# Transposing x by DMA in place of TensorE and ScalarE in a recurrent block with an FP4 feed-forward part

## The chip, the core and the metric

The kernel runs on one core of a Trainium2 chip. The metric is the device time of one execution in microseconds (us). The engines are named as the profile names them: PE (TensorE; PEld is its weight load), DVE (VectorE), ACT (ScalarE), POOL (GpSimd) and SP (SyncE, which here only issues DMAs). They run their own instruction streams and meet at semaphores.

## The reference, cut to what matters

The input u has 8 sequences of 1024 rows of 256 features, so 8192 rows. Everything starts from the layer-normalised input xn.

```
x  = u
xn = layernorm(x)
s  = causal_conv(xn, k) + xn * D          # k: 128 taps for each of 256 features, from Lambda, dt, W
q(v) = blockwise FP4 round trip of v      # blocks of 16: scale = max|v| / 6, round to the FP4 grid
h  = silu(q(xn) @ q(w_gate).T) * (q(xn) @ q(w_up).T)      # 704 wide
g  = silu(q(h) @ q(w_down).T)
out = x + s * g
```

## The kernel before, in words

The 8192 rows are 64 tiles of 128 rows. A step of the main loop works on a pair of tiles, so there are 32 pairs, and one step more at the end to drain the pipeline (`NP = 32`; `it` is the step). Row tiles lie with rows on the partitions.

In step `it` the engines do the following.

- DVE quantises. It takes the block maxima (`largest`, L926) of 1920 columns at once: h of pair it-1 (two tiles of 704) and x of pair it+2 (two tiles of 256). Then come the scales (L933, L937), the reciprocals (L941), the division by the scale (`inverse`, L949), the two rounding passes (L963, L968), and the products with the scale in two f16 parts, high and low: `h_parts` (L1000) writes `hilo`, `x_parts` (L976) writes `xhl`. Between them it multiplies silu(gate) by up twice, `h_mult` (L992), for tiles 2it and 2it+1.
- PE takes the parts with rows on partitions and has to transpose them before they can be the weights of a product. `h_transpose` (L1365) does it for h, 11 blocks of 128x128 a tile. `x_transpose` (L1344) does it for x, 8 blocks a pair, from `xhl` into PSUM. `gate_up` (L1356) is 18 matmuls a tile, `down` (L1374, L1376) 17 a tile.
- ACT copies the transposed blocks from PSUM: `h_copy` (L688) and `x_copy` (L683, into `xT`). It also computes silu (L693, L697), squares for the rounding (L708), normalises x (`x_norm`, L676), and in the first quarter normalises and splits the convolution's copy of u (`a_scale` L659, `a_high` L670).
- POOL makes the scale tables that `h_parts` and `x_parts` read (`tables`, L516 to L534; semaphore `tb_p`), and in steps 0 to 7 the low parts of u (`a_low`, L539; it needs `a_high`'s result through `a_hi`).

The causal convolution is a Toeplitz product on PE, `conv` (L1389, L1393). A group is 8 features in two halves of 24 matmuls. It starts at step 8 (`S_CONV`), because it needs u's high and low parts of all 64 tiles. From step 8 to step 28 an even step has two groups and an odd step one. The Toeplitz blocks of a half are read from a padded copy of the filter in DRAM (`kpad`) by one DMA of 512 KB, `load_t` (L449), into one of two buffers `tpl`; the DMA of half n waits until half n-2 is done (`cv_h`). The filter itself gets into `kpad` by 16 small DMAs, `store_filter` (L442).

The order of the work is written out by hand in each engine's stream; there is no scheduler. SP's stream is in order too, so a DMA that waits holds up those behind it. SP issues, per step, the load of a pair of x (`load_x`, L405), in steps 0 to 6 a copy of one sequence from u to the output in DRAM (`copy_input`, L455), and from step 8 on the `load_t`s.

Before step 1 there is a set-up: the filter and the quantised, transposed weights are made, and pairs 0 and 1 go through by hand (`gate_up(0, ...)` and `gate_up(1, ...)`, L1433 and L1444; `weights_out`, L817, copies the transposed weights from PSUM).

In the lines below, `x_hl` counts finished products of `x_parts`, `x_tp` PE's transposes of x, `x_tc` ACT's copies of them, `gu_p` finished `gate_up`s, `h_v` finished `h_mult`s.

```
def x_copy(p, par):                         # ACT
    act.wait_ge(x_tp, p + 1)
    after(act, gu_p, p * 2 - 2)
    nc.scalar.copy(xT[par], p_xT).then_inc(x_tc, 1)
```

Of the kernel before, what the change touches and what calls it, by code (L numbers as in the profile page):

```python
# [17 lines left out]
P = 128  # L18
# [51 lines left out]
def build(nc, u, u_rev, D, Lre, Lim, logdt, Wre, Wim, wg, wu, wd, out):  # L70
# [5 lines left out]
    with ExitStack() as ctx:  # L76
# [149 lines left out]
        x_tc = sem("x_tc")  # L226
        t_in = [sem(f"t_in{i}") for i in range(2)]
# [173 lines left out]
        def _(sp):  # L401
# [36 lines left out]
            def store_filter():  # L438
                sp.wait_ge(k_split, 3)
                for part, src in enumerate((kh, kl)):  # L440
                    for a in range(8):
                        sp.dma_start(  # L442
                            bass.AP(kpad, part * 3 * P + P - 1 + 16 * a, [[16 * 6 * P, 16], [6 * P, 16], [1, 16]]),
                            src[a:P:FA, :].rearrange("p (g b) -> p g b", b=16)).then_inc(k_dram, 16)
# [21 lines left out]
            sp.wait_ge(k_dram, 16 * 16)  # L466
            sp.wait_ge(w_ca, 13)
            load_t(0, 0)
            sp.wait_ge(x_hl, 2 * S_CONV + 4)
            load_t(1, 1)  # L470
            with sp.Fori(0, PAIRS - 1) as q:
                for par in range(2):
                    load_x(q * 2 + (S_CONV + par + 3), 1 - par)
                    for k in range(4 - 2 * par):
                        load_t(q * 6 + (4 * par + k + 2), k % 2)
            for it in range(S_TAIL - 2, NP - 3):
                load_x(it + 3, (it + 1) % 2)
                for n in range(2 * groups_before(it) + 2, min(2 * groups_before(it + 1) + 2, H // 4)):
                    load_t(n, n % 2)
            for n in range(2 * groups_before(NP - 3) + 2, H // 4):  # L480
                load_t(n, n % 2)
# [8 lines left out]
        def _(pool):  # L490
# [140 lines left out]
            for it in range(NP + 1):  # L631
                tables(it, it < NP - 2, it >= 1)
                if it == 1:
                    pool.wait_ge(k_split, 2)
                    nc.gpsimd.tensor_tensor(kl, kt, kh, ALU.subtract).then_inc(k_split, 1)
                some_stores()
                if it < NP - 2:
                    pool.wait_ge(x_hl, 2 * (it + 3))
                elif it < NP:
                    pool.wait_ge(hl_v, it)  # L640
                if it < S_CONV:
                    a_low(it * 2)
                    a_low(it * 2 + 1)
# [10 lines left out]
        def _(act):  # L654
# [68 lines left out]
            def step(it, par, x, xt, xn, gu, ch, td, a2=False, cv=0, c0=None, td1=True, late=False, more=None):  # L723
# [14 lines left out]
                if xt:  # L738
                    x_copy(it + 1, 1 - par)
# [8 lines left out]
                if more is not None:  # L748
                    a_scale(more, 2)
# [113 lines left out]
            weights_out(range(8, 11))  # L863
            a_scale(15, 0, 2)
# [3 lines left out]
            x_copy(1, 1)  # L868
            weights_out(range(11, 13))
# [7 lines left out]
            for it in range(1, PEEL):  # L877
                step(it, it % 2, True, True, True, True, True, it >= 2, a2=True, td1=it >= 3, late=it == 1,
                     more=15 if it == 3 else None)
            with act.Fori(0, (S_CONV - PEEL) // 2) as q:  # L880
                for par in range(2):
                    step(q * 2 + (PEEL + par), par, True, True, True, True, True, True, a2=True)
# [605 lines left out]
```

## Time and profile before

| | us |
|---|---|
| time, median of 3 runs | 563.04 (562.21 to 564.03) |
| the profiled execution's own time | 563.28 |
| its span, first to last instruction | 561.5 |
| busy: PE, DVE, ACT, POOL | 478.2, 531.4, 404.7, 220.2 |

The profile is of one execution. The granted clock of PE was 0.977 of full speed in the mean over the span. Busy times of PE are modelled at their ends, so a busy PE is not one at its peak. Steps are read off DVE's stream: each begins with one L926.

### The profile page before, as it was taken

The numbers are of one execution on the slowest core, as the hardware profiler recorded it, in microseconds if no ns is written. First come the engines' busy times: TensorE is split into PE (matmuls) and PEld (weight loads), VectorE is DVE, ScalarE is ACT, GpSimd is POOL, SyncE is SP. The second block draws the span as 40 slices with busy tenths as digits, with TensorE's granted clock in tenths as the row PEclk, the third lists the DMA queues.
The fourth block names the chain that finished last, engine by engine and source line by source line (L and its number), as shares of the span: only waits on it lengthen the run. The fifth ranks groups of instructions, "written<-read, shape, count | busy, mean of one in ns | idle before, by whom it ended". The sixth has DMA issues, their size and how long they took to land.

```text
span 561.5 us, 13319 instructions
## 1 busy us (share of the span) xinstructions
PE 478.2 (85%) x4981; PEld 332.7 (59%) x4981; DVE 531.4 (95%) x685; ACT 404.7 (72%) x571; POOL 220.2 (39%) x328
## 2 busy tenths in 40 slices
PE   0003487689989999999999999999999999999996
PEld 0000444255555567777777777777777777776675
DVE  6999999899999999999999999999999999999987
ACT  6959789879888876666766666666666767666554
POOL 1399832845544541111111111133332333337770
PEclk9999859799999999999999999999999999999999
DMA  5990005152221046253535353435353544426998
GB/s 164 351 321 1 1 20 187 23 175 95 95 94 54 5 134 187 77 171 94 152 99 147 96 160 97 140 95 168 95 169 95 144 122 126 139 76 134 191 175 178
DMA packets 101956, 70.82 MB, mean 126 GB/s; under 512 B 8864, under 2 KB 101536, under 8 KB 101792
## 3 DMA queue, kind: packets, MB, share of 16 engines
q1 hardware_dynamic: 94624, 62.73, 38.0%
q0 software_dynamic: 7280, 7.34, 8.6%
q8 instruction: 40, 0.66, 0.5%
q14 instruction: 12, 0.10, 0.1%
HBM read 61.28 MB, written 16.12 MB: 138 GB/s over the span
## 4 chain that ended last, share of the span: by engine, by line
PE 62%; DVE 26%; issue 6%; ACT 3%; POOL 2%; DMA 0%; SPq 0%; DVEq 0%; ACTq 0%; POOLq 0%
PE ps L1356 32%; PE ps L1374 10%; PE ps L1376 5%; PE ps L1365 5%; PE ps L1389 4%; PE ps L1393 4%; DVE work L968 3%; DVE work L1052 3%; DVE work L963 2%; DVE sm L926 2%; DVE work L992 2%; PE ps L1344 2%; DVE xh L1030 2%; DVE work L1000 1%; DVE work L976 1%
## 5 line engine op out<-in xcount | busy, mean ns | idle before, releaser
L1356 PE MATMUL ps<-wgu,work 128*128 128x512 f16 (+1 forms) x1152 | 243.9, 367 | 15.2 <-DVE work L992 15.0
L1356 PEld LDWEIGHTS ps<-wgu,work 128*128 128x128 f16 x1152 | 110.2, 99 | 126.6 <-issue 14.0
L693 ACT ACTIVATE work<-ps,con 128x704 f32<-128x704 f32 x64 | 54.3, 848 | 96.4 <-PE ps L1356 96.3
L1374 PE MATMUL ps<-wdh,work 128*128 128x256 f16 x704 | 87.2, 272 | 0.3 <-ACT work L688 0.2
L688 ACT COPY work<-ps 128x1408 f16<-128x1408 f16 x64 | 84.9, 1327 | 2.8 <-PE ps L1365 2.7
L549 POOL TENSOR_TENSOR gbuf<-gbuf,xh 128x256 f32<-128x256 f32 (+1 forms) x42 | 37.8, 930 | 94.0 <-DVE work L976 86.8
L963 DVE SCALAR_TENSOR_TENSOR work<-work 128x960 f32<-128x960 bf16 (+2 forms) x67 | 72.5, 1119 | 0.3 <-ACT work L708 0.2
L949 DVE TENSOR_TENSOR work<-work,ps 128x960 f32<-128x960 f32 (+2 forms) x67 | 71.4, 1105 | 1.2
L968 DVE SCALAR_TENSOR_TENSOR work<-work 128x1920 f16<-128x1920 bf16 (+3 forms) x36 | 69.7, 1936 | 1.2
L1374 PEld LDWEIGHTS ps<-wdh,work 128*128 128x128 f16 x704 | 65.3, 98 | 7.6 <-ACT work L688 0.4
L926 DVE TENSOR_REDUCE sm<-work 128x120 f32<-128x1920 f32 (+2 forms) x33 | 68.0, 2059 | 1.3
L708 ACT ACTIVATE work<-work 128x960 bf16<-128x960 f32 (+2 forms) x67 | 61.9, 960 | 3.4 <-DVE work L949 2.8
L1000 DVE TENSOR_TENSOR work<-work,sm 128x1408 f16<-128x1408 f16 (+1 forms) x66 | 54.9, 873 | 8.6 <-DVE work L968 5.0
L516 POOL TENSOR_SCALAR sm<-sm 128x2 int32<-128x2 int32 x32 | 8.5, 265 | 138.6 <-DVE sm L937 138.6
L992 DVE TENSOR_TENSOR work<-work,ps 128x704 f32<-128x704 f32 x64 | 56.4, 881 | 5.6 <-ACT work L693 5.5
L539 POOL TENSOR_TENSOR xh<-gbuf,xh 128x1024 f16<-128x1024 f32 x16 | 38.8, 2445 | 47.1 <-ACT xh L670 26.6
L697 ACT ACTIVATE gbuf<-ps,sm 128x256 f32 (+1 forms) x64 | 30.3, 474 | 32.9 <-PE ps L1376 32.8
L1365 PE MATMUL ps<-id,work 128*128 128x128 f16 x704 | 49.8, 219 | 4.5 <-DVE work L1000 4.3
L1376 PE MATMUL ps<-wdl,work 128*128 128x256 f16 x384 | 52.4, 273 | 0.0
L1365 PEld LDWEIGHTS ps<-id,work 128*128 128x128 f16 x704 | 43.2, 98 | 12.8 <-DVE work L1000 7.0
L1389 PE MATMUL ps<-xh,work 128*128 128x64 f16 x768 | 50.3, 192 | 0.0
L1393 PE MATMUL ps<-xh,work 128*128 128x56 f16 x768 | 50.1, 191 | 0.0
(156 smaller groups left out, 685.7 us busy)
## 6 DMA issues: line engine op xcount, KB each, us to landing
work<-kpad SPq DMA_DIRECT2D x64, 512.0 KB, 3.8
gbuf<-u_rev SPq DMA_DIRECT2D x4, 2048.0 KB, 18.7
work<-L_attn_u SPq DMA_DIRECT2D x32, 256.0 KB, 3.4
out<-gbuf POOLq DMA_DIRECT2D x7, 1024.0 KB, 11.5
work<-L_attn_u SPq DMA_DIRECT2D x1, 1024.0 KB, 5.5
out<-gbuf SPq DMA_DIRECT2D x3, 256.0 KB, 3.0
work<-L_ffn_w_down SPq DMA_DIRECT2D x1, 704.0 KB, 6.6
work<-L_ffn_w_gate SPq DMA_DIRECT2D x1, 640.0 KB, 4.6
```

Of the source, the lines that this page charges most:

```text
L688: nc.scalar.copy(hT[par], src).then_inc(hT_a, 1)
L926: own.mark(V.tensor_reduce(bm[:, cols], by_blk[pp][:, cols], AX_X, ALU.max, apply_absolute_value=True))
L949: V.tensor_tensor(v, v, sc, ALU.mult).then_inc(v_v, 1)
L963: own.mark(V.scalar_tensor_tensor(v, d_bf[:, c], C0, v, ALU.add, ALU.subtract))
L968: return V.scalar_tensor_tensor(r_f16[:, c], d_bf[:, c], C0, by_blk[pp][:, c], ALU.add, ALU.subtract)
L992: V.tensor_tensor(vb[par][:, I * t:I * t + I], sg, p_gu[:, I:2 * I], ALU.mult).then_inc(h_v, 1)
L1356: last = T.matmul(p_gu[:, a:b], xT[par][:, t, c, :], wgu[:, part, c % 2, a:b], start=(n == 0), stop=(n == len(todo) - 1))
L1365: last = T.transpose(dst[:, c, :], hilo[par][:, t, c * P:c * P + P], id16[:])
L1374: T.matmul(dst, hT[t][:, c, :], wdh[:, c, :], start=(c == 0), stop=False)
L1376: last = T.matmul(dst, hT[t][:, c, :], wdl[:, c, :], start=False, stop=(c == RT - 1))
L1389: T.matmul(dst, tpl[half][:, 2 * c + tp, 0:P], col[:, xp, :], start=(n == 0), stop=False)
L1393: last = T.matmul(dst1, tpl[half][:, 2 * c + tp, P:2 * P], before, start=False, stop=(n == 2))
```

## The change

x is no longer transposed by PE and copied by ACT, except for pair 0. SP issues a transposing DMA from `xhl` to `xT` for pair it+1 in its part of step it (`x_transpose` on SP, for pairs 1 to 31). It waits for the products of x (`x_hl`) and for the `gate_up`s that still read that `xT` buffer (`gu_p`). `gate_up` waits for the DMA (`x_td`, one semaphore for each of the two buffers) in place of `x_tc`, and so does `x_parts` before it overwrites `xhl`, in place of `x_tp`. SP's loop over steps is written out. The 16 stores of the filter go out four each in SP's steps 2 to 5, each four behind the transposing DMA of their step.

In the set-up ACT copies the last two blocks of transposed weights before `silu_gate(1)`; the two halves of `a_scale(15)` become one in step 2, so `a_high(0)` and `a_high(1)` stand right behind `silu_gate(1)`. PE transposes these two blocks before `gate_up(1)`. POOL's subtraction for the filter's low part stands behind its wait for x of step 1.

```
@@ sync
+            def x_transpose(p):
+                sp.wait_ge(x_hl, p * 2 + 2)
+                after(sp, gu_p, p * 2 - 2)
+                sp.dma_start_transpose(xT[p % 2].rearrange("p t c k -> p (t c) k"),
+                                       xhl[p % 2].rearrange("p t c -> p (t c)")).then_inc(x_td[p % 2], 16)
...
-            for it in range(PEEL):
-                load_x(it + 3, (it + 1) % 2)
-                if it == 2:
-                    store_filter()
-                copy_input(it)
-            for it in range(PEEL, S_CONV):
-                load_x(it + 3, (it + 1) % 2)
-                copy_input(it)
             sp.wait_ge(k_pad, 32)
...
+            for it in range(NP - 1):
+                if it < NP - 3:
+                    load_x(it + 3, (it + 1) % 2)
+                if it == 0:
+                    sp.wait_ge(k_all, 1)
+                if it == S_CONV - 1:
+                    sp.wait_ge(k_dram, 16 * 16)
+                    sp.wait_ge(w_ca, 13)
+                    load_t(0, 0)
+                x_transpose(it + 1)
+                if 2 <= it < 6:
+                    store_filter(it // 2 - 1, it % 2 * 4)
+                if it < S_CONV:
+                    copy_input(it)
+                if it == S_CONV:
+                    load_t(1, 1)
+                if it >= S_CONV:
+                    for n in range(2 * groups_before(it) + 2, min(2 * groups_before(it + 1) + 2, H // 4)):
+                        load_t(n, n % 2)
@@ gpsimd
                 tables(it, it < NP - 2, it >= 1)
-                if it == 1:
-                    pool.wait_ge(k_split, 2)
-                    nc.gpsimd.tensor_tensor(kl, kt, kh, ALU.subtract).then_inc(k_split, 1)
                 some_stores()
                 if it < NP - 2:
                     pool.wait_ge(x_hl, 2 * (it + 3))
                 elif it < NP:
                     pool.wait_ge(hl_v, it)
+                if it == 1:
+                    pool.wait_ge(k_split, 2)
+                    nc.gpsimd.tensor_tensor(kl, kt, kh, ALU.subtract).then_inc(k_split, 1)
@@ scalar, step
+                if more is not None:
+                    a_scale(more)
...
-                if xt:
-                    x_copy(it + 1, 1 - par)
...
-                if more is not None:
-                    a_scale(more, 2)
@@ scalar, set-up
-            weights_out(range(8, 11))
-            a_scale(15, 0, 2)
+            weights_out(range(8, 13))
             square(0, 1, True, False, 0)
             x_norm(3, 1)
             silu_gate(1)
-            x_copy(1, 1)
-            weights_out(range(11, 13))
             a_high(0, 2)
@@ vector, x_parts
-                after(dve, x_tp, p - 1)
+                if isinstance(p, int) and p < 3:
+                    after(dve, x_tp, p - 1)
+                else:
+                    dve.wait_ge(x_td[par], (p - 2 + par) * 8)
@@ tensor, gate_up
-                    pe.wait_ge(x_tc, first)
+                    if first == 1:
+                        pe.wait_ge(x_tc, 1)
+                    else:
+                        pe.wait_ge(x_td[par], (first - 1 + par) * 8)
@@ tensor, step
-                if x:
-                    x_transpose(it + 1, 1 - par)
@@ tensor, set-up
-            gate_up(1, 1, 0, None)
-            pe.wait_ge(con_ok, 1)
-            x_transpose(1, 1)
             pe.wait_ge(w_ca, 9)
             transposed_down(3)
             pe.wait_ge(w_ca, 10)
             transposed_down(4)
+            gate_up(1, 1, 0, None)
```

How the streams move, at the places that matter. Rows name the line, the operation, output and inputs, and in brackets the semaphores that it waits for; `ps` is PSUM, `work` the scratch area that holds `xhl`, `xT`, `hilo` and `tpl`.

PE, a step with convolution, from the last matmuls of its first `gate_up` to the first half of a group, before:

```order
L1356 MATMUL ps<-wgu,work 128x512 x2
L1356 MATMUL ps<-wgu,work 128x384
L1344 MATMUL ps<-id,work 128x128 [waits hT_a,x_tc,x_hl]
L1344 MATMUL ps<-id,work 128x128 x7
L1389 MATMUL ps<-xh,work 128x64 [waits cv_e,t_in0,a_lp]
L1389 MATMUL ps<-xh,work 128x64 x2
L1393 MATMUL ps<-xh,work 128x8x7 x3
```

The same place now:

```order
L1360 MATMUL ps<-wgu,work 128x512 x2
L1360 MATMUL ps<-wgu,work 128x384
L1391 MATMUL ps<-xh,work 128x64 [waits cv_e,t_in0,a_lp]
L1391 MATMUL ps<-xh,work 128x64 x2
L1395 MATMUL ps<-xh,work 128x8x7 x3
```

The eight transposes and their three waits are gone, and the convolution follows the `gate_up` directly.

SP, from the last `copy_input` to the second step with convolution, before (the stream is then a loop, so registers stand between):

```order
L455 DMA out<-L_attn_u 16x16384
L405 DMA work<-L_attn_u 128x2x256 [waits x_r]
L449 DMA work<-kpad 128x8x256 [waits w_ca,k_dram,k_pad]
L449 DMA work<-kpad 128x8x256 [waits x_hl]
L471 UNCONDITIONAL_BRANCH
L471 ISA
L405 ISA [waits x_r]
L405 DMA work<-L_attn_u 128x2x256
```

The same place now:

```order
L456 DMA out<-L_attn_u 16x16384
L406 DMA work<-L_attn_u 128x2x256 [waits x_r]
L450 DMA work<-kpad 128x8x256 [waits w_ca,k_dram]
L462 DMA_TRANSPOSE work<-work 128x8x128 [waits gu_p,x_hl]
L406 DMA work<-L_attn_u 128x2x256 [waits x_r]
L462 DMA_TRANSPOSE work<-work 128x8x128 [waits gu_p,x_hl]
L450 DMA work<-kpad 128x8x256
L450 DMA work<-kpad 128x8x256 [waits cv_h] x4
```

In each step one transposing DMA stands behind the step's `load_x` and ahead of its `load_t`s.

ACT, the end of the set-up, from the first `silu_gate` to the splitting of the filter, before:

```order
L693 ACTIVATE work<-ps,con 128x704 [waits gu_p,w_h,w_lo]
L822 COPY wdh<-ps 128x1024 [waits w_tr] x2
L822 COPY wdh<-ps 128x768 [waits w_tr]
L659 ACTIVATE gbuf<-gbuf,sm 128x256 x2
L708 ACTIVATE work<-work 128x512 [waits v_v,x_hl]
L676 ACTIVATE work<-work,nmr,rstd 128x256 [waits x_in1]
L676 ACTIVATE work<-work,nmr,rstd 128x256
L693 ACTIVATE work<-ps,con 128x704 [waits h_v,gu_p]
L683 COPY work<-ps 128x1024 [waits x_tp]
L822 COPY wdl<-ps 128x1024 [waits w_tr]
L822 COPY wdl<-ps 128x512 [waits w_tr]
L670 ACTIVATE xh<-gbuf 128x4x128x2 [waits w_ca,k_max,a_xs]
```

The same place now:

```order
L696 ACTIVATE work<-ps,con 128x704 [waits gu_p,w_h,w_lo]
L823 COPY wdh<-ps 128x1024 [waits w_tr] x2
L823 COPY wdh<-ps 128x768 [waits w_tr]
L823 COPY wdl<-ps 128x1024 [waits w_tr]
L823 COPY wdl<-ps 128x512 [waits w_tr]
L711 ACTIVATE work<-work 128x512 [waits v_v,x_hl]
L679 ACTIVATE work<-work,nmr,rstd 128x256 [waits x_in1]
L679 ACTIVATE work<-work,nmr,rstd 128x256
L696 ACTIVATE work<-ps,con 128x704 [waits h_v,gu_p]
L673 ACTIVATE xh<-gbuf 128x4x128x2 [waits w_ca,k_max,a_xs]
```

`a_high(0)` (the last row of each) now follows the second `silu_gate` with nothing between.

## Rows read from the trace of the kernel before

**Rows 1.** Page, part 1: busy time and share of each engine.

```profile
PE 478.2 (85%) x4981; PEld 332.7 (59%) x4981; DVE 531.4 (95%) x685; ACT 404.7 (72%) x571; POOL 220.2 (39%) x328
```

**Rows 2.** Windows: stretch, length; busy PE, PEld, DVE, ACT, POOL; PE's clock, DMA share.

```profile
124.57:196.67 72.10, 65.03 (x500) 41.86 (x500) 69.91 (x76) 65.28 (x94) 38.24 (x46) 1.00 0.22 73
225.62:518.58 292.96, 292.30 (x3404) 212.04 (x3401) 281.09 (x301) 198.28 (x270) 78.74 (x174) 1.00 0.45 124
```

**Rows 3.** Timeline of DVE, steps 10 to 30: start, length, line [idle before it].

```profile
225.62 2.15 DVE L926 TENSOR_REDUCE sm<-work 128x120 f32<-128x1920 f32 x1
...
298.54 2.15 DVE L926 TENSOR_REDUCE sm<-work 128x120 f32<-128x1920 f32 x1
304.72 0.89 DVE L992 TENSOR_TENSOR work<-work,ps 128x704 f32<-128x704 f32 x1 [0.36 <-ACT work L693]
313.50 2.15 DVE L926 TENSOR_REDUCE sm<-work 128x120 f32<-128x1920 f32 x1
319.23 0.88 DVE L992 TENSOR_TENSOR work<-work,ps 128x704 f32<-128x704 f32 x1
324.64 1.69 DVE L1000 TENSOR_TENSOR work<-work,sm 128x1408 f16<-128x1408 f16 x2 [0.20 <-DVE work L968]
327.84 2.15 DVE L926 TENSOR_REDUCE sm<-work 128x120 f32<-128x1920 f32 x1
...
518.58 1.62 DVE L926 TENSOR_REDUCE sm<-work 128x88 f32<-128x1408 f32 x1
```

**Rows 4.** Chain of waits, from step 16: start, length, line and instructions.

```profile
313.56 0.61 PE ps L1365 x11
314.17 3.56 PE ps L1356 x18
317.74 0.45 PE ps L1344 x8
318.18 0.09 PE ps L1389 x3
...
318.89 1.20 PE ps L1374 x11
320.10 0.66 PE ps L1376 x6
...
342.86 0.61 PE ps L1365 x11
```

**Rows 5.** Timeline of DVE, steps 1 and 2.

```profile
92.93 2.15 DVE L926 TENSOR_REDUCE sm<-work 128x120 f32<-128x1920 f32 x1
...
105.90 2.17 DVE L1000 TENSOR_TENSOR work<-work,sm 128x1408 f16<-128x1408 f16 x2 [1.68 <-POOL sm L531]
...
109.65 2.15 DVE L926 TENSOR_REDUCE sm<-work 128x120 f32<-128x1920 f32 x1
```

**Rows 6.** Timeline of POOL, step 1.

```profile
95.10 4.85 POOL L539 TENSOR_TENSOR xh<-gbuf,xh 128x1024 f16<-128x1024 f32 x2 [6.12 <-ACT xh L670]
99.91 1.14 POOL L516 TENSOR_SCALAR sm<-sm 128x2 int32<-128x2 int32 x1
...
105.23 0.64 POOL L531 TENSOR_TENSOR sm<-sm 128x240 f16<-128x240 f32 x1
```

**Rows 7.** Timeline of ACT, end of the set-up.

```profile
91.35 0.99 ACT L683 COPY work<-ps 128x1024 f16<-128x1024 f16 x1
...
93.86 2.08 ACT L670 ACTIVATE xh<-gbuf 128x1024 f16<-128x1024 f32 x2
```

**Rows 8.** Timeline of PE: `gate_up(2)` and `gate_up(3)`.

```profile
92.97 3.73 PE L1356 MATMUL ps<-wgu,work 128*128 128x512 f16 x18 [1.94 <-DVE work L992]
...
99.60 5.24 PE L1356 MATMUL ps<-wgu,work 128*128 128x512 f16 x18 [2.46 <-DVE work L992]
```

**Rows 9.** Page, part 6: DMA issues, KB each, us from issue to landing.

```profile
work<-kpad SPq DMA_DIRECT2D x64, 512.0 KB, 3.8
```

**Rows 10.** DMA issues by line: the padding's zeros, 512 rows of 254 bytes.

```profile
kpad<-work SPq DMA_DIRECT2D x1, 127.0 KB, 6.8
```

More of the change, by code:

```diff
@@ L226, in build @@
         x_tc = sem("x_tc")
+        x_td = [sem(f"x_td{i}") for i in range(2)]
         t_in = [sem(f"t_in{i}") for i in range(2)]
@@ L436, in _, with store_filter @@
             load_x(2, 0)
-            def store_filter():
+            def store_filter(part, a0):
                 sp.wait_ge(k_split, 3)
[L440 to L444, printed above, removed]
+                src = (kh, kl)[part]
+                for a in range(a0, a0 + 4):
+                    sp.dma_start(
+                        bass.AP(kpad, part * 3 * P + P - 1 + 16 * a, [[16 * 6 * P, 16], [6 * P, 16], [1, 16]]),
+                        src[a:P:FA, :].rearrange("p (g b) -> p g b", b=16)).then_inc(k_dram, 16)
             def load_t(n, par):
@@ L721, in y_copy, with step @@
                                      scale=con[:, C_CONV:C_CONV + 1]).then_inc(cv_e, 1)
-            def step(it, par, x, xt, xn, gu, ch, td, a2=False, cv=0, c0=None, td1=True, late=False, more=None):
+            def step(it, par, x, xn, gu, ch, td, a2=False, cv=0, c0=None, td1=True, late=False, more=None):
                 if td:
@@ L877, in _ @@
             for it in range(1, PEEL):
-                step(it, it % 2, True, True, True, True, True, it >= 2, a2=True, td1=it >= 3, late=it == 1,
-                     more=15 if it == 3 else None)
+                step(it, it % 2, True, True, True, True, it >= 2, a2=True, td1=it >= 3, late=it == 1,
+                     more=15 if it == 2 else None)
             with act.Fori(0, (S_CONV - PEEL) // 2) as q:
                 for par in range(2):
-                    step(q * 2 + (PEEL + par), par, True, True, True, True, True, True, a2=True)
+                    step(q * 2 + (PEEL + par), par, True, True, True, True, True, a2=True)
             act.wait_ge(con_ok, 1)
@@ L885, in _ @@
                 for par in range(2):
[L886 removed]
+                    step(q * 2 + (S_CONV + par), par, True, True, True, True, True, cv=2 - par, c0=q * 3 + 2 * par)
             for it in range(S_TAIL, NP - 2):
[L888 to L890 removed]
+                step(it, it % 2, True, it < NP - 3, True, True, True, cv=groups_of(it), c0=groups_before(it))
+            step(NP - 2, 0, False, False, True, True, True)
+            step(NP - 1, 1, False, False, True, True, True)
             h_copy(NT - 4, 0)
@@ L1358, in gate_up, with h_transpose @@
                 last.then_inc(gu_p, 1)
-            def h_transpose(n, t, par, dst=p_hT, copied=None):
+            def h_transpose(n, t, par, dst=p_hT):
                 after(pe, hT_a, n if dst is p_hT else n - 1)
-                if copied is not None:
-                    pe.wait_ge(x_tc, copied)
                 for c in range(NC11):
@@ L1399, in keep_running, with step @@
                     T.matmul(ps[:, 1024:1024 + H], id16[:], wdh[:, n % NC11, :], start=True, stop=True)
-            def step(it, par, x, gu, td, cv=0):
+            def step(it, par, gu, td, cv=0):
                 if td:
                     pe.wait_ge(hl_v, it - 1)
-                    h_transpose(it * 2 - 4, 0, par, copied=min(it + 1, NP))
+                    h_transpose(it * 2 - 4, 0, par)
                 if gu:
                     gate_up(it * 2, 0, par, it + 1)
-                if x:
-                    x_transpose(it + 1, 1 - par)
                 if cv:
@@ L1418, in step @@
                 if td:
-                    h_transpose(it * 2 - 3, 1, par, copied=it + 2 if x else None)
+                    h_transpose(it * 2 - 3, 1, par)
                 if cv == 2:
@@ L1450, in _ @@
             transposed_down(4)
+            gate_up(1, 1, 0, None)
             for it in range(1, NP - 1):
-                step(it, it % 2, True, True, it >= 2, groups_of(it) if it >= S_CONV else 0)
-            step(NP - 1, 1, False, True, True)
-            step(NP, 0, False, False, True)
+                step(it, it % 2, True, it >= 2, groups_of(it) if it >= S_CONV else 0)
+            step(NP - 1, 1, True, True)
+            step(NP, 0, False, True)
             down(NT - 3, 1, p_dn2)
```

20 lines of the change are left out of this document (removed).

## The prediction, made before the changed kernel ran

> **What bounds the kernel now.** I read the page's busy shares first, then windows over the stages, then DVE's timeline (how long is a step?) and the chain of waits (who sets it?), and last POOL, ACT and PE in the set-up. The page alone points at DVE: 95% busy against PE's 85% [rows 1]. The windows split that. In steps 3 to 7 (124.57 to 196.67) the five steps take 72.10 us, 14.42 each, with DVE busy 97% and PE 90% [rows 2]: DVE is the bound there, and PE work taken away saves nothing. From 225.62 to 518.58, steps 10 to 29, PE is busy 292.30 of 292.96 us and DVE 96% [rows 2]: PE is the bound, but DVE is close behind.
>
> How close is what the estimate hangs on. DVE's timeline shows steps in turns of two lengths: step 16 from 313.50 to 327.84 is 14.34 us, step 15 from 298.54 to 313.50 is 14.96. In the long one `h_mult` waits 0.36 us for silu, and so for a late `gate_up`; in the short one there is no wait before it [rows 3]. So 14.34 us is DVE's own length. A pair of steps takes 292.96 / 10 = 29.30 us now, and 28.68 would be DVE's floor. The chain of waits says the same from the other side: it runs on PE alone from 313.56 to 342.86, 29.30 us with no gap [rows 4].
>
> **The convolution steps.** PE loses the eight transposes, 0.45 us a step [rows 4], so its pair falls from 29.30 to 28.40 us. That is under DVE's 28.68, so DVE becomes the bound and the gain is 29.30 - 28.68 = 0.62 a pair, not 0.90: over ten pairs 292.96 - 20 x 14.34 = 6.2 us.
>
> Does DVE really run free, when PE has only 0.28 us a pair to spare and its two steps are unequal? An even step has two groups. A half of a group is eight rows of 0.09, so 0.71 us; `h_transpose` is 0.61, `gate_up` 3.56, `down` 1.86 [rows 4]. The even step is then 2 x 0.61 + 2 x 3.56 + 2 x 1.86 + 4 x 0.71 = 14.9 us on PE, the odd one two halves less, 13.5. If DVE's even step begins at S, `gate_up` may start at S + 0.1 (the last `h_mult` frees the PSUM bank), its `h_transpose` being done before, and PE ends the step at S + 14.4. DVE's odd step begins at S + 14.34; PE transposes h for 0.61, runs `gate_up` for 3.56, silu takes 0.85, so DVE can multiply 5.2 us after its step began. It wants to at 319.23 - 313.50 = 5.73 [rows 3]. There is 0.5 us to spare, so the 0.36 us waits go. The second `gate_up` of a step has more room.
>
> **ACT and DVE.** ACT loses a copy of 1.0 us a step [rows 7]. It is busy 68% in these steps [rows 2] and is not what anyone waits for, so I count nothing. In its loop DVE's wait before `x_parts` is now for a number worked out in a register of its own. The nearest row for what that can cost is the 0.20 us of idle before `h_parts`, which also waits for a computed number behind its own last result [rows 3]. Lower bound 0, upper bound 0.20 a step over 26 looped steps, 5.2 us. I take 0: the number can be worked out while the second product of `h_parts` runs, and that takes 0.85 of the 1.69 us [rows 3].
>
> **The transposing DMA.** No DMA of this kind is in the trace. It moves 256 KB in 1024 rows of 256 bytes. The nearest rows are `load_t`, 512 KB in 1024 rows of 512 bytes, 3.8 us to landing [rows 9], and the padding's zeros, 512 rows of 254 bytes, 6.8 us for half the bytes [rows 10], which would give 13.6. Lower end 1.9 (half of `load_t`), upper end 13.6; I take 4, because `load_t` has the same number of rows and runs in the same steps on the same queue, while the zeros went out beside 8 MB of u. It is issued when `x_parts` is done, one `h_mult` (0.9) before DVE's next step, or when the last `load_t` of the step is off SP, which is PE's end of the step. Its reader, `gate_up` of the next step but one, comes a whole step (14.3 us) later. At 4 us nobody waits, and even 13.6 would just do.
>
> The tighter customer is the next `load_t`, which lies behind it in the queue. In an even step the first `load_t` can go when the first half is done, S + 0.1 + 3.56 + 0.71 = S + 4.4, which is 5.3 us after the DMA was issued at S - 0.9. Its Toeplitz blocks are wanted by the second group, S + 11.1, so it has 6.7 us for its 3.8, 2.9 to spare. The transposing DMA may therefore hold the queue for 8.2 us before PE waits.
>
> Two pages of the Trainium skill bear on this and disagree. "VectorE: DVE Perf Modes", section "The three transpose paths", gives 1309 ns for one 128x128 block by DMA and 390 ns on TensorE, and its rules prefer TensorE where PSUM will do; if the eight blocks went one after the other, that would be an estimated 10.5 us, 2.3 past the point, and would speak against the change. In this trace a block costs PE 0.45 / 8 = 0.056 us in a stream [rows 4], far less than the page's figure, so its figures are not those of a stream. "Advanced Engine Details and Errata", section "X-Bar Transpose (TRN2)", says that such DMAs are as fast as regular ones, which would put it at or below the 4 us taken. No run here yet shows which holds.
>
> **The filter's stores and POOL.** The 16 stores move from one block to four steps, behind transposing DMAs; `kpad` is first read in step 7's part of SP, more than a step after the last of them. Nothing.
>
> **The set-up.** Step 1 takes 16.72 us and step 2 follows at 109.65 [rows 5]; steps 3 to 7 average 14.42 [rows 2], so step 1 has 2.3 us too much. 1.68 of them are DVE waiting for POOL's tables before `h_parts` [rows 5]. POOL is late because `a_low`, 4.85 us, starts only at 95.10, when `a_high(0)` is through ACT, and the tables come behind it from 99.91 to 105.87 [rows 6]. ACT begins `a_high` at 93.86, after `x_copy` at 91.35 and the two weight copies [rows 7]. Now it begins at about 91.4, 2.4 us earlier. POOL then starts its tables at 97.5 and, at the 5.96 us that they take now, ends by 103.5, before DVE asks at 105.90 - 1.68 = 104.2. So the 1.68 us go. The weight copies land in ACT's idle time and before `silu_gate(1)`; PE's `gate_up(1)` begins some 1.2 us later behind the two weight blocks and its silu is then just in time. What replaces the stall: `gate_up(2)` now waits for the first transposing DMA, issued at about 87.8; at 4 us it lands before the 92.97 at which `gate_up(2)` starts now [rows 8], and DVE needs its result only 1 us after it is there. The rest of the 2.3 us is DVE work slowed beside POOL's, which partly goes. I take 2.0; ends 0 and 2.8.
>
> **Sum.** 6.2 + 2.0 = 8.2 us off the profiled execution's 563.28 (the closing steps, with DVE waiting once for silu, I leave at nothing): 555.1. The median of the runs is 0.24 lower, so 554.9 us.
>
> **Rivals.** (a) *The DMA holds the queue* (slower). By the zeros' row it would take 13.6 us, 5.4 past the 8.2 at which it decides. PE would wait that once a pair: 28.40 + 5.4 = 33.8 against 29.30, ten times, 45 us more, less 2: about 606 us. Just past the point, at 9.2 us, PE's pair is 29.4 and nothing is gained but the set-up. For it: rows of 256 bytes, a kind of DMA that no row shows. Against: `load_t` with as many rows in 3.8. At the page's estimated 10.5 us it would be 2.3 late, a pair of 30.7, and some 575 us.
> (b) *DVE pays for the computed wait*, 0.1 us in each of 26 steps: 2.6 less, 557.5; at 0.20, 560.1. For it: DVE is the bound everywhere afterwards, so nothing hides it.
> (c) *The set-up gives nothing back.* PE's clock: `gate_up(3)` took 5.24 us after 2.46 us of idle, `gate_up(2)` 3.73 after 1.94 [rows 8]; the same instructions at 1.2 and 2.4 GHz in part. PE now has less work before `gate_up(2)` and a longer gap; if that one is slow too, DVE waits about 0.6, and the same in step 2: gain 6.2 or less, 556.9.
> (d) *PE stays the bound* because the slack of 0.28 us a pair isn't usable, and pairs stay at 29.0 or above: 3 + 2 off, 558; with the set-up lost too, no change.
>
> **How the numbers follow.** Forecast 0.62, (a) 0.10, (b) 0.12, (c) 0.10, (d) 0.06. The forecast's own range is 552.5 to 557: the set-up's 0 to 2.8 and half a microsecond of spread. To leave out no more than 2 in 10 I go up to 560.0, which takes in (b), (c) and most of (d), and down to 552.0; (a) is left out. A run of this kernel tells a difference from none at about 0.3%, 1.7 us. Slower by more than that is (a), 0.10 less the part of it that ends near today's time, plus a little for what I didn't see: 0.09. Within it: 0.05. Faster: 0.86.
>
> **What would show it.** Right: DVE's steps 10 to 29 all at 14.34 us, no `h_mult` waiting for silu, PE busy about 97% there with its gaps before `gate_up`; L1000 in step 1 without the wait for POOL; the transposing DMA at 3 to 5 us, `load_t` still near 4. Wrong: convolution matmuls waiting for `work<-kpad` or `gate_up` for the transposing DMA (a), even and odd steps both a little over 14.34 with an idle before `x_parts` (b), `gate_up(2)` over 5 us (c), pairs still uneven (d).

## The result, and the profile after

The changed kernel takes 554.79 us in the median of four runs (554.51 to 555.17), where the kernel before takes 563.5 in the four runs made beside them (562.21 to 564.03). The ratio is 0.9853, with a 95% interval of 0.9838 to 0.9867, so the change is worth 1.5%. The forecast was 554.9. The profiled execution's own time is 554.96 us, and its span is 553.2. Of the experiments' executions below, one of e1's twelve took 1768 us and is in no ratio, and two of e11's seven took 558.2 and 559.5 where its other five lie within 0.5 us.

The page's first part, to be read beside [rows 1]. DVE keeps its 685 instructions and about its busy time, while PE, ACT and POOL lose some:

```profile
PE 466.3 (84%) x4733; PEld 318.7 (58%) x4733; DVE 529.0 (96%) x685; ACT 379.6 (69%) x540; POOL 218.1 (39%) x328
```

Windows over step 1 and over steps 10 to 29, with the columns of [rows 2]:

```profile
93.11:107.94 14.83, 10.29 (x47) 4.81 (x47) 14.15 (x16) 10.14 (x17) 8.72 (x11) 0.85 0.41 124
223.22:509.77 286.55, 284.67 (x3238) 202.64 (x3235) 279.27 (x301) 183.12 (x250) 77.77 (x174) 1.00 0.57 142
```

The last window took 292.96 us before and takes 286.55 now. DVE's busy time in it has fallen by only 1.8 us, from 281.09 to 279.27, while its share rose from 96% to 97.5%. PE still shows 99%, with 166 recorded matmuls fewer. Its idle time in the window rose only from 0.66 to 1.88 us, which is 0.19 a pair, and as the ends of matmuls are modelled this is a rough figure. The share says little on which engine sets the step. The stretches between starts on DVE say it.

DVE's timeline, steps 16 and 17, to be read against [rows 3]:

```profile
309.18 2.15 DVE L924 TENSOR_REDUCE sm<-work 128x120 f32<-128x1920 f32 x1
...
314.92 0.88 DVE L993 TENSOR_TENSOR work<-work,ps 128x704 f32<-128x704 f32 x1
...
320.33 1.69 DVE L1001 TENSOR_TENSOR work<-work,sm 128x1408 f16<-128x1408 f16 x2 [0.20 <-DVE work L966]
...
323.53 2.15 DVE L924 TENSOR_REDUCE sm<-work 128x120 f32<-128x1920 f32 x1
...
337.84 2.15 DVE L924 TENSOR_REDUCE sm<-work 128x120 f32<-128x1920 f32 x1
```

The step's first instruction, `largest`, stands 14.35 and 14.31 us from the next one. `h_mult` (L993) begins 5.74 us after it, with no wait in brackets, and 5.73 us after it in the next step. The long step of [rows 3], in which it stood 0.36 us for silu, is gone. The short one has stayed as it was.

The chain of waits, with its shares by engine from the page's fourth part:

```profile
DVE 61%; issue 22%; PE 11%; ACT 3%; DVEq 1%; POOL 1%; DMA 0%; SPq 0%; ACTq 0%; POOLq 0%
```

Its pieces over one step, first and last, in the place of [rows 4]:

```profile
309.18 2.16 DVE sm L924
...
323.53 2.17 DVE sm L924
```

Where [rows 4] run on PE from `h_transpose` to `h_transpose`, these run on DVE from `largest` to `largest`. The bound has moved from PE to DVE.

The span is 8.3 us shorter. Cut at DVE's step starts, the difference is made up like this:

| Stretch | Before | After | Difference | Forecast |
|---|---|---|---|---|
| start to step 3 | 124.57 | 122.65 | -1.9 | -2.0 |
| steps 3 to 9 | 101.05 | 100.57 | -0.5 | 0 |
| steps 10 to 29 | 292.96 | 286.55 | -6.4 | -6.2 |
| steps 30 and 31 up to the last `largest` | 24.03 | 23.77 | -0.3 | 0 |
| from there to the end (the span is given to 0.1) | 18.9 | 19.7 | +0.8 | 0 |

In the last of these stretches DVE does its work in the same time. Its last instruction starts 16.2 us after that `largest` in both traces (542.61 before, 533.54 after):

```profile
558.85 0.42 DVE L1249 TENSOR_TENSOR gbuf<-gbuf,work 128x256 f32<-128x256 f32 x1
...
549.77 0.42 DVE L1250 TENSOR_TENSOR gbuf<-gbuf,work 128x256 f32<-128x256 f32 x1
```

Behind it stand only the last stores. The span ends 2.2 us after DVE's last instruction before (561.5 - 559.3) and 3.0 us after it now (553.2 - 550.2). That is the 0.8.

The first row of the table, the set-up, sets one execution against one. In e7, e8, e9 and e10, whose programs are the same up to here, step 3 begins at 123.02, 123.29, 123.31 and 122.80 us, where it begins at 122.65 in this trace. So by traces the gain is 1.3 to 1.9 us, and this trace is the best of five.

The set-up, on the three engines of the forecast. First DVE, against [rows 5], with the window of step 1 before:

```profile
92.93:109.65 16.72, 10.20 (x55) 4.90 (x55) 14.80 (x16) 14.03 (x21) 12.66 (x11) 0.89 0.28 92
...
99.28 0.89 DVE L993 TENSOR_TENSOR work<-work,ps 128x704 f32<-128x704 f32 x1 [0.34 <-ACT work L696]
...
104.68 1.69 DVE L1001 TENSOR_TENSOR work<-work,sm 128x1408 f16<-128x1408 f16 x2
```

The 1.68 us that `h_parts` waited for POOL are gone, and a new wait of 0.34 for silu has come. Of the 1.89 us by which step 1 is shorter, 1.24 are idle time of DVE and 0.65 its busy time, which fell from 14.80 to 14.15: `h_parts`, for one, takes 1.69 us and no longer the 2.17 of [rows 5]. POOL, against [rows 6]:

```profile
92.94 4.83 POOL L542 TENSOR_TENSOR xh<-gbuf,xh 128x1024 f16<-128x1024 f32 x2 [3.78 <-ACT xh L673]
97.74 0.22 POOL L519 TENSOR_SCALAR sm<-sm 128x2 int32<-128x2 int32 x1
...
99.57 0.64 POOL L534 TENSOR_TENSOR sm<-sm 128x240 f16<-128x240 f32 x1
```

`a_low` starts 2.16 us earlier, because `a_high(0)` does on ACT, at 91.71 where [rows 7] have 93.86:

```profile
91.71 2.05 ACT L673 ACTIVATE xh<-gbuf 128x1024 f16<-128x1024 f32 x2
```

PE's `gate_up(2)` and `gate_up(3)`, against [rows 8]:

```profile
93.16 5.20 PE L1360 MATMUL ps<-wgu,work 128*128 128x512 f16 x18 [2.47 <-DVE work L993]
...
100.22 3.74 PE L1360 MATMUL ps<-wgu,work 128*128 128x512 f16 x18 [1.87 <-DVE work L993]
```

The slow one is now `gate_up(2)`, with 5.20 us for the 18 matmuls that took 3.73 before, and DVE's 0.34 us are the wait for its silu. The window over it has the clock in the third column from the end, 0.71 of full speed:

```profile
93.11:98.40 5.29, 5.20 (x18) 2.04 (x18) 5.18 (x6) 1.46 (x4) 5.15 (x4) 0.71 0.98 297
```

The transposing DMAs and, for e9 below, the closing transfers, from the DMA issues (KB each, where given, and median us to landing), beside [rows 9]:

```profile
work<-kpad SPq DMA_DIRECT2D x64, 512.0 KB, 4.1
...
work<-L_attn_u SPq DMA_DIRECT2D x1, 1024.0 KB, 12.7
out<-gbuf SPq DMA_DIRECT2D x3, 256.0 KB, 4.0
...
work<-work SPq DMA_TRANSPOSE x31, 3.2
```

They land after 3.2 us in the median: 18 of the 31 after 3.0 to 3.7, 12 after 4.7 to 6.6 and the last one, in step 30, after 10.7. The mean is 4.2. Even the last is in time, landing at 519.6 for a step that starts at 521.3. The `load_t` behind them rose only from 3.8 to 4.1.

### The profile page after: what moved, and what is told of

Its sections match the earlier page's. It is cut to its first block, busy times and chain, and to the rows that moved or that the text cites. A ratio compares the mean times of both kernels' runs of the same rounds, so it can differ in the third digit from the quotient of the medians.

```text
span 553.2 us, 12607 instructions
## 1 busy us (share of the span) xinstructions
PE 466.3 (84%) x4733; PEld 318.7 (58%) x4733; DVE 529.0 (96%) x685; ACT 379.6 (69%) x540; POOL 218.1 (39%) x328
## 4 chain that ended last, share of the span: by engine, by line
DVE 61%; issue 22%; PE 11%; ACT 3%; DVEq 1%; POOL 1%; DMA 0%; SPq 0%; ACTq 0%; POOLq 0%
DVE work L966 11%; DVE sm L924 10%; DVE work L961 9%; PE ps L1360 7%; DVE work L993 6%; DVE ps L939 4%; DVE work L977 3%; DVE work L1053 3%; DVE work L947 3%; DVE work L1001 2%; DVE xh L1031 2%; DVE sm L931 1%; PE ps L1376 1%; DVE xh L1021 1%; PE ps L1367 1%
## 5 line engine op out<-in xcount | busy, mean ns | idle before, releaser
L993 DVE TENSOR_TENSOR work<-work,ps 128x704 f32<-128x704 f32 x64 | 56.3, 880 | 2.0 <-ACT work L696 1.8
L1391 PEld LDWEIGHTS ps<-xh,work 128*128 128x128 f16 x768 | 43.8, 96 | 5.2 <-POOL xh L542 0.9
## 6 DMA issues: line engine op xcount, KB each, us to landing
work<-L_attn_u SPq DMA_DIRECT2D x1, 1024.0 KB, 12.7
```

The source lines that it names most:

```text
L993: V.tensor_tensor(vb[par][:, I * t:I * t + I], sg, p_gu[:, I:2 * I], ALU.mult).then_inc(h_v, 1)
L1391: T.matmul(dst, tpl[half][:, 2 * c + tp, 0:P], col[:, xp, :], start=(n == 0), stop=False)
```

## The experiments

Twelve kernels ran. Eleven are edits of the changed kernel, and `setup_only` (e4) is an edit of the kernel before. A ratio is always to the kernel before.

**e1 and e5, TensorE's work alone.** This asks whether the gain in the steps is PE's relief and nothing else. Eight constant transposes of the identity go back on PE in e1, two in e5. x still comes by DMA.

```diff
+                if 1 <= it < NP - 1:
+                    after(pe, hT_a, it * 2 - 3)
+                    for n in range(8):       # 2 in e5, 16 in e6
+                        T.transpose(p_xT[:, n // 4 % 2, n % 4, :], id16[:], id16[:])
```

> The changed kernel, with eight transposes of a constant block put back on TensorE in steps 1 to 30, where x's stood; ScalarE's copy stays out and x still comes by DMA. Theory (TensorE was the bound in the convolution steps, and its 0.45 us a step is what was gained): pairs of steps back from 28.65 to 29.30 us, 561.2 us (560.5 to 561.8). Rival (the gain came from ScalarE's missing copy, or from x being there a step early): 554.8.

Measured: 561.87 us, ratio 0.9971 (0.996 to 0.9983). DVE's timeline in e1:

```profile
295.86 2.15 DVE L924 TENSOR_REDUCE sm<-work 128x120 f32<-128x1920 f32 x1
302.11 0.89 DVE L993 TENSOR_TENSOR work<-work,ps 128x704 f32<-128x704 f32 x1 [0.44 <-ACT work L696]
...
310.80 2.15 DVE L924 TENSOR_REDUCE sm<-work 128x120 f32<-128x1920 f32 x1
```

The long step of 14.94 is back with its wait for silu, and steps 10 to 29 take 292.96 us, exactly as before. Nothing of ACT's part, of the DMAs or of the set-up was undone. So the 6.4 us of the steps are PE's eight transposes. What e1 still has over the kernel before, 1.6 us, is about the set-up's gain.

> The changed kernel with two constant transposes a step on TensorE where x's stood. Theory (TensorE now has 28.65 - 28.40 = 0.25 us to spare in a pair, and two times 0.11 us fit in): no change, 554.8 us (554.3 to 555.5). Rival (every TensorE instruction still costs its own time): 20 x 0.11 = 2.2 more, 557.0.

Measured: 555.16 us, 0.9843 (0.9826 to 0.9859), with steps of 14.34 and 14.32. Two blocks on PE in each step, 0.11 us, cost nothing. So PE's time to spare can be used.

**e6, sixteen transposes.** If DVE's 28.65 us a pair is a floor and PE's length a straight line that crosses it, sixteen must cost what eight cost and 0.45 a step more.

> The changed kernel with sixteen constant transposes a step on TensorE. Theory (over the spare 0.25 us every us on TensorE costs a us): a pair is 28.40 + 1.80 = 30.20 us, ten pairs 15.5 more, 570.3 us (569 to 572). Rival (latencies between the engines add to it): 575 or more.

Measured: 571.26 us, 1.0133 (1.0116 to 1.015), with steps of 14.41 and 15.78, 30.19 a pair. DVE's wait in the long step has grown to 1.27 us:

```profile
305.97 0.89 DVE L993 TENSOR_TENSOR work<-work,ps 128x704 f32<-128x704 f32 x1 [1.27 <-ACT work L696]
```

The pair goes 28.65 (none), 28.66 (two), 29.30 (eight), 30.19 (sixteen): flat at first, and 0.89 between eight and sixteen, which is the 16 x 0.056 of the added blocks. Taken back from 29.30 at that slope, PE's own pair without transposes is 28.4, as forecast, and DVE's floor is met at about two blocks a step.

**e2, ScalarE's copy put back.** A copy of the same size, of constant data, at the same place on ACT, and `silu_gate` behind it.

```diff
+                if gu and xn:
+                    act.wait_ge(h_v, it * 2 + 1)
+                    nc.scalar.copy(sg.bitcast(F16)[:, 0:1024].rearrange("p (c k) -> p c k", c=8),
+                                   id16[:].rearrange("p (o k) -> p o k", o=1).to_broadcast([P, 8, P])).then_inc(x_dm, 1)
```

> The changed kernel, with a copy of 128x1024 f16 (about 1 us) put back on ScalarE in steps 1 to 28, at the old place of x's copy; its result is not used. Theory: ScalarE is busy two thirds and nobody waits for it, so 554.8 us (554.3 to 555.6). Rival (its copy was in the way of silu or of the convolution's copies): 557 or more.

Measured: 554.89 us, 0.9847 (0.9827 to 0.9866). The window of steps 10 to 29:

```profile
223.57:510.24 286.67, 284.72 (x3238) 202.22 (x3235) 279.38 (x301) 198.76 (x269) 77.54 (x174) 1.00 0.57 142
```

ACT is busy 198.76 us in it, as much as before the change (198.28 in [rows 2]), and the window is 0.12 us longer. ACT's copy was worth nothing, as counted.

**e3 and e4, the set-up.** e3 is the changed kernel with the orders of u's high parts, of the weight copies, of `gate_up(1)` and of the filter's subtraction as before. e4 is the kernel before with these orders alone changed.

```diff
 # e3, core of the edit
-            weights_out(range(8, 13))
+            weights_out(range(8, 11))
+            a_scale(15, 0, 2)
...
+            weights_out(range(11, 13))
...
-                     more=15 if it == 2 else None)
+                     more=15 if it == 3 else None)
```

> The changed kernel with the set-up's order of before (weight copies and half a_scale ahead of a_high, transposed_down behind gate_up(1), GpSimd's subtraction first); x comes by DMA. Theory (the first step's gain is GpSimd's tables coming in time, because a_high starts earlier): a_high starts 1.5 us later than now, 0.7 earlier than before, so the tables are late by 0.5 to 1 us: 555.7 us (555.0 to 556.8). Rival (the first step gained because TensorE's and ScalarE's work on x is gone there): 554.8.

Measured: 556.56 us, 0.9875 (0.9854 to 0.9896), 1.8 us over the changed kernel. POOL and DVE are as in [rows 5, 6] again, in small. POOL:

```profile
94.23 4.84 POOL L542 TENSOR_TENSOR xh<-gbuf,xh 128x1024 f16<-128x1024 f32 x2 [5.31 <-ACT xh L673]
```

and DVE's `h_parts` behind it:

```profile
104.94 2.17 DVE L1003 TENSOR_TENSOR work<-work,sm 128x1408 f16<-128x1408 f16 x2 [0.53 <-POOL sm L534]
```

The wait is 0.53 and not 1.68 us, since `a_low` begins at 94.23 and not at 95.10: the x copy of [rows 7] is gone from ahead of `a_high` on ACT. So a part of the gain here, some 0.9 us of POOL's start, comes with the transposing DMA. The 1.8 us aren't all the tables' either. Against the changed kernel, step 1 of e3 is 0.98 us longer (15.81), with the wait and the slower `h_parts`, and step 2 is 0.60 longer (15.31), with a wait of 0.82 for silu behind a slow `gate_up(4)`. Such a wait stands in e2 too (1.19 in step 2), which has the new orders, so it isn't shown to come from the old ones.

> The kernel before with only the set-up's new order; x is still transposed by TensorE and copied by ScalarE. Theory: a_high starts 1.5 us earlier than before, the 1.7 us wait for GpSimd's tables goes, 1.8 us less: 561.7 us (561.0 to 562.5), and steps 10 to 29 stay at 29.30 us a pair. Rival: the set-up's order alone does nothing, 563.5.

Measured: 561.48 us, 0.997 (0.9958 to 0.9982). Steps 1 and 3 begin here:

```profile
92.41 2.15 DVE L924 TENSOR_REDUCE sm<-work 128x120 f32<-128x1920 f32 x1
...
103.95 1.70 DVE L998 TENSOR_TENSOR work<-work,sm 128x1408 f16<-128x1408 f16 x2
...
121.93 2.15 DVE L924 TENSOR_REDUCE sm<-work 128x120 f32<-128x1920 f32 x1
```

The orders alone take the wait away. Step 3 begins 2.6 us before the 124.57 of the kernel before, but takes 15.20 us itself where it took 14.23, so that 1.75 us are left at step 10. Steps 10 to 29 keep their 14.35 and 14.94. The two halves add up: e4 is 2.0 us under the kernel before, the changed kernel 7.1 under e1, and together that is 9.1 where 8.7 was measured for both.

**e7 and e8, how long SP's queue may be held.** Rival (a) was a condition, a queue held for more than 8.2 us. In even steps one (e7) or two (e8) stores of 1.41 MB follow the transposing DMA, from a buffer that nobody writes to one that nobody reads.

```diff
+                if 10 <= it <= 28 and it % 2 == 0:
+                    for n in range(1):       # 2 in e8
+                        sp.dma_start(spill[it * 1 + n], wgu[:, :, :, :].rearrange("p a k c -> p (a k c)")).then_inc(x_sp, 16)
```

> The changed kernel with one store of 1.41 MB from SBUF to an unused DRAM buffer behind the transposing DMA in the ten even steps 10 to 28; it holds the queue. Theory (the next load of filter blocks has 8.2 us from the issue of the transposing DMA before TensorE waits; the two DMAs together hold it for about 8): 0 to 3 us more, 554.8 to 558. Rival (what lies ahead in the queue does not delay a load): 554.8 here and in the run with two stores.

Measured: 553.93 us, 0.9828 (0.9812 to 0.9845). SP's timeline:

```profile
308.76 1.23 SPq L464 DMA_TRANSPOSE work<-work  x1
310.03 0.58 SPq L480 DMA_DIRECT2D spill<-wgu  x1
314.14 2.92 SPq L452 DMA_DIRECT2D work<-kpad  x2
```

This store lands 5.2 us after its issue, 310.03 + 5.2 - 308.76 = 6.5 us after the transposing DMA went out. In the ten pairs it is 6.5 to 8.4 us, and the first `load_t` lands 9.0 to 10.3 us after the transposing DMA. That costs nothing. The first `load_t` goes out 5.4 us after the transposing DMA, where 5.3 was forecast.

> As the run before with two stores, 2.8 MB. Theory: the queue is held for about 14.5 us, 6 past the point, once a pair in ten pairs: 60 us more, 615 us (590 to 640). Rival: 554.8.

Measured: 572.88 us, 1.0169 (1.0152 to 1.0186): slower, but far less than expected. SP's timeline:

```profile
315.11 1.23 SPq L464 DMA_TRANSPOSE work<-work  x1
316.38 1.06 SPq L480 DMA_DIRECT2D spill<-wgu  x2
320.54 9.74 SPq L452 DMA_DIRECT2D work<-kpad  x3
```

The landing of the 20 stores:

```profile
DMA to landing us min/median/max: 5.2/7.9/10.5
```

And what PE's weight loads waited for in the steps (us in all, times, longest), with the wait of this pair:

```profile
PEld ps L1397 <- DMA work<-kpad: 17.8, 12, 2.4
...
329.01 0.14 PEld L1397 LDWEIGHTS ps<-xh,work 128*128 128x128 f16 x3 [1.93 <-DMA work<-kpad]
```

The median of the landings is no store's own: the first of a pair lands after 5.2 to 6.7 us, the second after 9.0 to 10.5. Counted from the transposing DMA the second is there after 10.9 to 12.4 us. I had assumed 14.5, and that is one part of the miss. The other is that `load_t` doesn't take its 3.8 us behind the last store: it lands only 1.5 to 3.4 us after it, 12.7 to 14.3 after the transposing DMA. In this pair that is 13.9 us (329.01 - 315.11).

PE asks for it at 329.01 - 1.93 = 327.08, which is 12.0 us after the transposing DMA. The forecast had 8.2 + 3.8 = 12.0. The price follows from there: the stretch from step 10 to step 29 is 303.3 us, 16.7 over the changed kernel's, so 1.7 a pair, between 0.9 and 3.5. So the mechanism and its point are right when the landing of `load_t` is the measure: 10.3 us cost nothing and 12.7 cost a wait. As a time for which the queue is held, the 8.2 us are only bounded, between 8.4 us that cost nothing in e7 and 10.9. That a transposing DMA which lands as late would have cost the same is argued; no run has one in these pairs.

**e9, the closing stretch.** It lost 0.8 us. In the changed kernel the load of u's last rows (1 MB) waits behind the last transposing DMA. e9 puts it ahead.

```diff
+                if it == NP - 2:
+                    sp.wait_ge(cv_h, H // 4)
+                    sp.dma_start(u_last, u_t[:, NT - 8:NT, :]).then_inc(u_in, 16)
...
-            sp.wait_ge(cv_h, H // 4)
-            sp.dma_start(u_last, u_t[:, NT - 8:NT, :]).then_inc(u_in, 16)
```

> The changed kernel with the last load of u (1 MB, for the closing sums) ahead of the last transposing DMA in SP's stream and no longer behind it. Theory (the tail lost 0.8 us because this load slid from 57 to 41 us before the end, into the time of GpSimd's accumulating stores, and the last stores land in 3.0 and no longer 2.2 us): 0.8 us less, 554.0 us. Rival (the landing varies by itself, or by the stores alone): 554.8.

Measured: 554.53 us, 0.9844 (0.9826 to 0.9862). The DMA issues:

```profile
work<-L_attn_u SPq DMA_DIRECT2D x1, 1024.0 KB, 5.5
out<-gbuf SPq DMA_DIRECT2D x3, 256.0 KB, 2.2
```

The load lands in 5.5 us instead of 12.7, the closing stores in 2.2 instead of 4.0, and the stretch takes 18.9 us, as before the change. The four traces with an early load (the kernel before, e4, e9, e12) have 18.9, 18.8, 18.9 and 19.2 us here. The ten with a late one have 18.9 (e7), 19.0 (e10), 19.3 to 20.4 (seven of them) and 21.2 (e11). The traces favour this cause, but they overlap, and the time can't tell e9 from the changed kernel, so it stays open.

**e10, DVE's loop written out.** Rival (b) said that DVE pays for waits on computed numbers. With steps 4 to 29 written out every number is a constant.

```diff
-                with dve.Fori(0, (s1 - s0) // 2) as q:
...
+                for it in range(s0, s1):
+                    step(it, it % 2, True, True, True)
```

> The changed kernel with VectorE's loop over steps 4 to 29 written out, so that its waits are for constants. Theory (VectorE is the bound, and 0.1 us of the 0.2 us before h_parts is the computed wait): 26 x 0.11 = 2.9 us less, 551.9 us (551.3 to 553). Rival (the wait is the instruction's own, or TensorE at 28.40 us a pair becomes the bound): 554.8, or 28.40 against 28.65, 2.5 less at most in the convolution steps.

Measured: 554.14 us, 0.9835 (0.9815 to 0.9855), 0.65 under the changed kernel, where 2.9 was expected. DVE's timeline:

```profile
320.45 1.69 DVE L1001 TENSOR_TENSOR work<-work,sm 128x1408 f16<-128x1408 f16 x2
...
322.73 0.88 DVE L993 TENSOR_TENSOR work<-work,ps 128x704 f32<-128x704 f32 x1
323.72 2.15 DVE L924 TENSOR_REDUCE sm<-work 128x120 f32<-128x1920 f32 x1
```

The 0.20 of idle before `h_parts` is gone, but `largest` now starts 323.72 - 322.73 - 0.88 = 0.11 us after `h_mult`'s end, where it was 0.04. The window of steps 10 to 29 is 285.92 us, 0.03 a step less. Most of what the row shows as idle comes back elsewhere; what adds it there is open.

**e11, filling PE's gap in the set-up.** Can small matmuls before step 1 keep `gate_up(2)` from being slow?

```diff
+            pe.wait_ge(w_ca, 13)
+            for n in range(36):
+                T.matmul(ps[:, 3072:3072 + P], id16[:], id16[:], start=True, stop=True)
```

> The changed kernel with 36 small matmuls of a constant block on TensorE between gate_up(1) and gate_up(2), written to an unused PSUM bank. Theory (gate_up(2) runs at 1.2 GHz after 2.5 us of idle, takes 5.2 us and lets VectorE wait 0.34 us in step 1): gate_up(2) back to 3.7 us, step 1 0.4 us shorter, 554.4 us. Rival (the clock was low for another reason, or gate_up(3) is slow in its place): 554.8.

Measured: 554.83 us, 0.9853 (0.9835 to 0.9871), no gain. PE's timeline, from the execution of 559.5 us, 4.7 over the median:

```profile
93.49 3.73 PE L1360 MATMUL ps<-wgu,work 128*128 128x512 f16 x18 [0.45 <-DVE work L993]
...
100.12 5.42 PE L1360 MATMUL ps<-wgu,work 128*128 128x512 f16 x18 [2.90 <-DVE work L993]
```

`gate_up(2)` has its full speed, and `gate_up(3)` is the slow one. That isn't shown to be the fill's doing, since e1 has the same with no fill, after an idle of 2.46 us ahead of either:

```profile
92.92 3.73 PE L1360 MATMUL ps<-wgu,work 128*128 128x512 f16 x18 [2.46 <-DVE work L993]
...
99.55 5.19 PE L1360 MATMUL ps<-wgu,work 128*128 128x512 f16 x18 [2.46 <-DVE work L993]
```

So which of the set-up's bursts runs slow isn't settled by the gap ahead of it alone. What a slow burst costs depends on where it falls: in this trace of e11 steps 2 and 3 take 15.56 and 15.93 us, with waits for silu, where the changed kernel's take 14.71 and 14.23.

**e12, the edits of e9, e10 and e11 together.**

> The three edits together: last load of u early, VectorE's loop written out, the 36 small matmuls. Theory: 0.8 + 2.9 + 0.4 less, 550.7 us (550.0 to 552.5).

Measured: 553.83 us, 0.9835 (0.9817 to 0.9852), not the 550.7 expected. It is 1.0 us under the changed kernel, and the two intervals overlap. No version here is shown to be better than the changed kernel.

## Why the prediction was right

**The bound and the sum (forecast's main step).** The floor of 14.34 us a step was read off the short step of [rows 3] and holds: 286.55 / 20 = 14.33. So 6.4 us came for 6.2. e1, e5 and e6 show that it is a floor and not a chance agreement, since the pair stays flat up to two blocks and then rises by 0.056 a block and step. The forecast took DVE's 0.62 us a pair and not PE's 0.90, which would have given 9.0 us; it rested on the two shares of [rows 2] lying close together. Rival (d), that the 0.28 us a pair can't be used, falls with e5. One sign named for a right forecast did not come: PE was to be busy about 97% in these steps and is at 99%. That was a slip, since the forecast's own 28.40 of 28.68 us are 99%.

**No gain from ACT.** Shown by e2.

**The computed wait, rival (b).** Taken at nothing, and right for `x_parts`: the trace shows no idle before it. Its upper end of 0.20 a step was read off an idle of the old wait, and e10 shows that taking all such waits away gives 0.03 a step.

**The transposing DMA and rival (a).** It was taken at 4 us, from `load_t`'s number of rows. It is 3.2 in the median and 4.2 in the mean, with one landing of 10.7. The zeros' row, the upper end, was the wrong relative. A regular DMA of the same 256 KB, x's own load, takes 2.9 in the same trace:

```profile
work<-L_attn_u SPq DMA_DIRECT2D x32, 256.0 KB, 2.9
```

The rule in "Advanced Engine Details and Errata", section "X-Bar Transpose (TRN2)", of the Trainium skill, that such DMAs are as fast as regular ones, agrees to within 0.3 us in the median. The estimate of 10.5 from "VectorE: DVE Perf Modes", section "The three transpose paths", doesn't hold for eight blocks in one DMA: 30 of the 31 land within 6.6 us, and the one landing of 10.7 stands in step 30, where plain DMAs are slow too (12.7 for u's last rows). The point, 12.0 us from the transposing DMA's issue to `load_t`'s landing, was worked out from [rows 3, 4, 9] alone. In e8 PE asks for the blocks at just that time, and e7 and e8 stand on its two sides. The step from there to rival (a)'s price, that `load_t`'s 3.8 us come whole behind whatever holds the queue, was too dear for e8: 60 us were expected and 18.1 came.

**The set-up.** 1.9 us came for 2.0 in the trace, where 1.3 to 1.9 is what five traces give, so the closeness is in part luck. e4 shows by time that the orders on ACT, PE and POOL give a gain of this size (2.0 us, 1.0 to 2.4 by its interval), and the lines of e3 and e4 that it goes through the wait for the tables. Two of its parts were off. The tables take 100.2 - 97.7 = 2.5 us and not the 5.96 taken over from [rows 6], so there was more margin than I saw. Rival (c) was right in that a slow `gate_up(2)` did come. In this trace it cost 0.34 in step 1 and not 0.6, and `gate_up(3)` was fast in exchange. Before, DVE waited 0.44 us for silu in step 2, and that wait is gone, so that no gain was lost. In other traces the wait is larger: 0.56 in step 1 (e8, e9), 1.19 in step 2 (e2). I had asked whether one more burst would be slow, and should have asked whether the slow one moves.

**What the sum left out.** Steps 3 to 9 gave 0.5 and steps 30 and 31 gave 0.3, while the closing stretch took 0.8. They nearly cancel, so the median agrees better than the terms do. For steps 30 and 31 the wait for silu is 0.97 us instead of 1.21. In steps 3 to 9 it is mostly step 5 that took 14.71 before and takes 14.34 now. Its idle time ahead of `h_parts` was 0.53 us, where the steps on its two sides have 0.21 and 0.20. A single long step of this kind stands in other kernels too (step 5 of e4 with 14.67, step 6 of e10 with 14.65), and its cause is open. The closing stretch is e9's question, open as well. The forecast left it at nothing, without asking what the load of u's last rows is queued behind and which transfers then run beside it.

## What to carry to other kernels

When two engines are both nearly always busy, take work off the one only as far as the other's own step length, and read that length off a step in which it waits for nothing. For an operation that no trace shows, work out the point from which its price decides: that point can be tested by holding the queue with a dummy store, whatever the price turns out to be, if the landings are read one by one and not as a median. PE's busy share was 99% or more both when it was the bound and when it no longer was. Dummy work added in several sizes measures the time to spare.

## What the runs showed of the hardware

- **A transposing DMA between two SBUF buffers** (128x1024 f16, 256 KB) lands in 3.2 us in the median (3.0 to 10.7), much like a plain one (2.9 for x's load), but its issue holds SP longer: 1.23 to 2.51 us, 1.26 in the median, against 0.36 to 0.40 for `load_t`:

```profile
308.38 1.23 SPq L462 DMA_TRANSPOSE work<-work  x1
313.76 0.36 SPq L450 DMA_DIRECT2D work<-kpad  x1
```

- **POOL's small operations slow down beside some of DVE's.** The tables' operation on 128x2 numbers takes 1.14 us in [rows 6], beside DVE's `round_a` and `round_b`, whose inputs all lie in SBUF. The same operation takes 0.22 us at 97.74 above, beside `inverse` with one input in PSUM. Another of this size took 2.00 us before, to the end of the DVE instruction beside it, and takes 0.19 now:

```profile
102.07 2.16 DVE L968 SCALAR_TENSOR_TENSOR work<-work 128x1920 f16<-128x1920 bf16 x1
...
102.28 2.00 POOL L521 TENSOR_SCALAR sm<-sm 128x2 int32<-128x2 int32 x1
```

"GPSIMD Engine Reference", section "Specifications", of the Trainium skill says that POOL shares its SBUF interfaces with DVE and contends with instructions of two SBUF inputs. The trace agrees, with a factor of five and of ten on these two. One case in the changed kernel's trace is not explained by it: at 536.2 the first of these operations takes 0.87 us beside `inverse`.

- **TensorE's clock.** The granted clock of step 1 is 0.85 in the changed kernel's trace. While `gate_up(2)` takes 5.20 us it is 0.71, and at full speed the same 18 matmuls take 3.73, so a part of them ran at the lower of the two levels, 1.2 and not 2.4 GHz. Of the bursts behind step 0, the first slow one is `gate_up(2)` in the changed kernel, in e3 and in e6 to e10. It is `gate_up(3)` in the kernel before, e1, e5 and e11, `gate_up(4)` in e2 and e12 with 6.0 us, and `gate_up(5)` in e4 with 5.4. The idle time ahead of `gate_up(2)` is 2.47 us in the changed kernel, where it is slow, and 2.46 in e1 and e2, where it is not.
